# Softmax maxima split on VectorE and moved from SBUF to SBUF, keys in four stored blocks, in a gated cross-attention layer with experts

## The chip, the cores and the metric

The kernel runs on one core of one Trainium2 chip. The metric is the device time of one execution in microseconds. A core has TensorE (PE), VectorE (DVE), ScalarE (ACT), GpSimd (POOL) and SyncE (SP), whose queue issues nearly all DMAs here.

## The reference

Sixteen sequences of 256 tokens with 128 features attend to 1601 context rows each, in 16 heads of depth 8; a mixture of eight experts follows. Both branches are added to x with a tanh gate.

```python
x = x + tanh(g_xattn) * attention(ctx, ctx, layernorm(x))      # qh, kh, vh: heads of 8
#   softmax(qh @ kh.T / sqrt(8)) @ vh, then the dense layer
x = x + tanh(g_ffn) * ffn(layernorm(x))
#   top 2 of 8 experts by sigmoid(x @ gate_W), gelu hidden layers of 64, plus a shared expert
```

## The kernel before

**Steps.** One step is half of a batch's heads: step s works on batch s // 2, eight heads, 256 queries; there are 32 steps. Float32 products of queries and keys are made with bf16 operands: each of q and k is split in three bf16 parts (value, rest, rest of the rest), and 48 rows of an operand tile hold six of their pairings (`KPART`, `QPART`). Two heads' operands lie at partitions 0 and 64 (`SIDE`).

**Two passes over the scores.** For the softmax's maximum, PE computes scores with queries on the partitions (L741, events S, 26 for each step) and DVE reduces them (L901, L904). From these DVE makes the negated maximum of each query and head (`neg_max`, L911). Then PE computes the scores again, transposed, with keys on the partitions (L757, events P, 26 pairs for each step). The negated maximum comes in as three more operand rows, 48 to 50 of each side of `q_op`. ACT takes the exponential of each (L573), PE multiplies with the values (L775, events V and W), and ACT copies the sums out (L581).

**The way of the maxima.** `neg_max` lies with tokens on the partitions; the operand rows need heads on rows and tokens along them. So in event T, PE transposes it (L697), ACT copies it to `nm_t` (L605), POOL splits it in three with four instructions (`split_maxima`, L469 to L475), SP writes the parts to HBM (L416), waits, and reads them back into the rows of `q_op` (L419). The first pair P of the next step waits for that. T of step s+1 stands in step s, after about 17 of its 26 pairs.

**Order.** PE, ACT and DVE each walk one list (`PLAN`, `ORDER`), one string for each phase s % 4. Score passes of step s+1, values of step s and s-1, and auxiliary units are woven in it: K (keys, L688, from `kctx`), V (values, L692, from `vctx`), QT and QP (queries), F (experts), D (dense layer). In the lists of phases 0 and 2 stand the four K units of batch b+2. In phase 0 the first comes at the head, ahead of P0, in phase 2 a little after it; the last comes after T.

**Keys and queries through HBM.** The projected keys `k_t` are split (POOL, four instructions on all 1601 columns, after the last K unit), stored six times over (`store_keys`, L397: 600, 400 and 200 KB for each half) and read back as rows of `k_op` (`load_operands`, L332). Queries go the same way with twelve stores for 512 tokens (L406).

**SP's list.** SP is one queue in program order, and it stops at each wait. In an odd step s it does: outputs of s-1, `store_keys` for b+2, `load_operands` for s+3 (once the stores have landed), key context for b+3 (L387), value context for b+2 (L387, once the last V unit of b+1 is done), maxima of s+1, and in phase 3 the query stores. In an even step: outputs, operands, the softmax's sums by way of HBM (L361, L367), in phase 2 the gates (L375, L381), maxima. Before the loop it issues the context of batch 0, all tokens and weights, `vctx`, the keys of batch 0, `kctx` of batch 1, the queries, the operands of step 0.

## Time and profile before

| what | value |
|---|---|
| median of 3 runs | 1435.47 us (1433.91 to 1437.52) |
| the profiled execution's own time | 1436.73 us |
| its span | 1434.9 us |
| busy, PE / ACT / DVE / POOL | 87% / 74% / 73% / 29% |
| mean granted TensorE clock | 0.902 |
| moved by DMA | 147.13 MB, 103 GB/s |

The span runs from the first to the last instruction of the program. The granted clock is 1.00 at TensorE's 2.4 GHz and 0.50 at 1.2 GHz. In the rows below, a row of the timeline has the start in us, the time that the merged instructions take, the engine, the line of the kernel, the operation with what it writes and reads, and in brackets how long the engine sat idle before it and what ended that.

### The profile page before, as it was taken

Reading aid. Unit: us, or ns where it says so; the run is one execution under the profiler, and the core shown is the slowest. Engines: PE = TensorE matmul, PEld = TensorE weight load, DVE = VectorE, ACT = ScalarE, POOL = GpSimd, SP = SyncE. Lnnn points to the kernel's source line nnn. Section 1 sums busy time; section 2 is a strip of 40 time slices with the busy share of each in tenths; the row PEclk is TensorE's granted clock in tenths of the full one; section 3 lists DMA queues with packets and bytes.
Section 4 is the critical chain, followed back from the end, with each engine's and each line's share of the span. In section 5 each row is a group of like instructions: output and inputs, shape, how many; then the busy total and the mean of one; then the engine's idle time right before and its main releaser. Section 6 shows DMA issues by size and latency. Waiting matters only on the chain.

```text
span 1434.9 us, 29778 instructions
## 1 busy us (share of the span) xinstructions
PE 1241.7 (87%) x11555; PEld 458.9 (32%) x11555; DVE 1049.3 (73%) x1208; ACT 1055.6 (74%) x1962; POOL 418.7 (29%) x309
## 2 busy tenths in 40 slices
PE   2448889798989999899989999799979999799855
PEld 1112323232323433243323333243323433243224
DVE  8477778587768888688868878688768868689001
ACT  1008879587978799688968789688968889689741
POOL 7242224051333215151424125051423205010111
PEclk6568999798988999899989999899989999899786
DMA  7673634636273653737273744637173744501101
GB/s 213 114 149 69 150 70 98 140 84 129 53 164 70 139 119 87 147 81 149 52 169 61 170 87 99 139 82 146 47 167 67 165 92 96 102 11 33 31 14 45
DMA packets 71390, 147.13 MB, mean 103 GB/s; under 512 B 13705, under 2 KB 37970, under 8 KB 71250
## 3 DMA queue, kind: packets, MB, share of 16 engines
q1 hardware_dynamic: 71250, 145.24, 47.4%
q8 instruction: 91, 1.49, 0.5%
q14 instruction: 49, 0.40, 0.1%
HBM read 88.30 MB, written 56.91 MB: 101 GB/s over the span
## 4 chain that ended last, share of the span: by engine, by line
PE 66%; DMA 14%; ACT 5%; DVE 4%; SPq 4%; POOL 3%; issue 2%; POOLq 0%; ACTq 0%; DVEq 0%
PE o_ps L775 26%; PE a_ps L757 15%; PE b_ps L741 11%; DMA m_dram<-nm_parts 10%; PE a_ps L688 4%; PE a_ps L692 4%; ACT probs L573 3%; PE b_ps L720 2%; DVE run_max L901 2%; SPq L406 2%; DMA q_op<-m_dram 1%; SPq L397 1%; PE a_ps L684 1%; PE b_ps L723 1%; DMA q_op<-q_dram 1%
## 5 line engine op out<-in xcount | busy, mean ns | idle before, releaser
L901 DVE TENSOR_REDUCE run_max<-b_ps 128x2 f32<-128x1024 f32 x768 | 899.4, 1218 | 249.4 <-PE b_ps L741 246.0
L573 ACT ACTIVATE probs<-a_ps 128x512 f32<-128x512 f32 (+1 forms) x1664 | 901.9, 594 | 144.3 <-PE a_ps L757 127.4
L775 PE MATMUL o_ps<-probs,v_op 128*32 128x256 f32 (+3 forms) x4928 | 505.8, 483 | 2.3 <-ACT probs L573 1.2
L757 PE MATMUL a_ps<-q_op,k_op 51*128 51x256 bf16 (+1 forms) x3328 | 338.1, 283 | 46.4 <-DMA q_op<-m_dram 25.6
L741 PE MATMUL b_ps<-k_op,q_op 48*128 48x512 bf16 (+1 forms) x2048 | 325.6, 350 | 37.5 <-DVE run_max L901 24.2
L757 PEld LDWEIGHTS a_ps<-q_op,k_op 51*128 51x128 bf16 (+1 forms) x3328 | 112.9, 97 | 373.5 <-ACT probs L573 307.3
L741 PEld LDWEIGHTS b_ps<-k_op,q_op 48*128 48x128 bf16 x2048 | 88.7, 96 | 208.2 <-DVE run_max L901 95.9
L775 PEld LDWEIGHTS o_ps<-probs,v_op 128*32 128x32 f32 (+1 forms) x4928 | 98.4, 109 | 176.4 <-issue 93.8
L509 POOL TENSOR_TENSOR attn<-num,den_all 128x256 f32<-128x256 f32 x16 | 11.6, 728 | 440.3 <-DMA den_all<-r_dram 440.3
L688 PE MATMUL a_ps<-kctx,wk_s 128*128 128x400 f32 (+1 forms) x128 | 81.4, 734 | 55.7 <-DMA kctx<-ctx_t 49.9
L469 POOL TENSOR_TENSOR nm_parts<-nm_t,one 8x256 bf16<-8x256 f32 x32 | 19.3, 602 | 360.5 <-ACT nm_t L605 360.5
L594 ACT ACTIVATE k_t<-a_ps,bk_s 128x401 f32<-128x401 f32 (+1 forms) x64 | 38.1, 597 | 106.7 <-PE a_ps L688 106.6
L692 PE MATMUL a_ps<-wv_s,vctx 128*128 128x128 f32 (+1 forms) x416 | 64.4, 294 | 0.0
L888 DVE SCALAR_TENSOR_TENSOR y_s<-b_ps,tgf,x_s 128x128 f32<-128x128 f32 x32 | 11.2, 349 | 71.3 <-PE b_ps L724 71.2
L599 ACT ACTIVATE v_op<-a_ps 128x512 f32<-128x512 f32 x64 | 32.9, 513 | 36.7 <-PE a_ps L692 36.3
L692 PEld LDWEIGHTS a_ps<-wv_s,vctx 128*128 128x128 f32 (+1 forms) x416 | 51.2, 192 | 20.8 <-issue 11.5
L469 POOL TENSOR_TENSOR k_parts<-k_t,one 128x1601 bf16<-128x1601 f32 x15 | 42.8, 2850 | 43.8 <-ACT k_t L594 43.8
L688 PEld LDWEIGHTS a_ps<-kctx,wk_s 128*128 128x128 f32 x128 | 25.9, 248 | 83.1 <-issue 61.0
L904 DVE TENSOR_REDUCE run_max<-b_ps 128x8 f32<-128x520 f32 x64 | 43.9, 696 | 10.3 <-PE b_ps L741 10.3
L471 POOL TENSOR_TENSOR k_t<-k_t,k_parts 128x1601 f32<-128x1601 f32 x15 | 48.5, 3230 | 1.2
L475 POOL TENSOR_TENSOR k_parts<-k_t,k_parts 128x1601 bf16<-128x1601 f32 x15 | 45.3, 3021 | 1.2
L473 POOL TENSOR_TENSOR k_parts<-k_t,one 128x1601 bf16<-128x1601 f32 x15 | 42.8, 2851 | 1.2
(100 smaller groups left out, 680.4 us busy)
## 6 DMA issues: line engine op xcount, KB each, us to landing
k_op<-k_dram SPq DMA_DIRECT2D x64, 600.4 KB, 9.5
k_dram<-k_parts SPq DMA_DIRECT2D x32, 600.4 KB, 6.0
kctx<-ctx_t SPq DMA_DIRECT2D x16, 800.5 KB, 12.5
vctx<-ctx_t SPq DMA_DIRECT2D x16, 800.5 KB, 11.8
k_dram<-k_parts SPq DMA_DIRECT2D x32, 400.2 KB, 7.0
o_dram<-o_s SPq DMA_DIRECT2D x32, 256.0 KB, 2.1
g_all<-g_dram SPq DMA_DIRECT2D x16, 512.0 KB, 6.4
k_dram<-k_parts SPq DMA_DIRECT2D x32, 200.1 KB, 6.7
```

The costliest lines, as they stand in the source:

```text
L469: pool.tensor_tensor(parts[0], whole, ones(whole, slice(0, whole.shape[0])), ALU.mult).then_inc(chain, 1)
L471: pool.tensor_tensor(whole, whole, parts[0], ALU.subtract).then_inc(chain, 1)
L473: pool.tensor_tensor(parts[1], whole, ones(whole, slice(0, whole.shape[0])), ALU.mult).then_inc(chain, 1)
L475: pool.tensor_tensor(parts[2], whole, parts[1], ALU.subtract).then_inc(chain, 1)
L573: act.activation(probs[0:keys, unit % PB, :], a_ps[at % AB][0:keys, :], ACT.Exp, scale=SCALE).then_inc(a_taken, 1)
L688: last = pe.matmul(bank[:, 0:n_keys], wk_s[:, :], kctx[:, k0:k0 + n_keys], start=True, stop=True)
L692: last = pe.matmul(bank[0:KEYS[t], 128 * (t % 4):128 * (t % 4) + 128], vctx[:, 128 * t:128 * t + KEYS[t]], wv_s[:, :], start=True, stop=True)
L741: last = pe.matmul(slot[:, side, to:to + n_keys], q_op[buf][rows, p, 128 * t:128 * t + 128], k_op[buf][rows, p, k0:k0 + n_keys], start=Tru ...
L757: last = pe.matmul(a_ps[(at + side) % AB][0:KEYS[t], SEQ * a:SEQ * a + SEQ], k_op[buf][rows, slot, 128 * t:128 * t + KEYS[t]], q_op[buf][r ...
L775: last = pe.matmul(o_ps[32 * j:32 * j + 32, cols], v_op[s // 2 % 2][0:KEYS[t], t, GP * (s % 2) + j, :], probs[0:KEYS[t], unit % PB, cols], ...
L901: dve.tensor_reduce(run_max[:, t, :, p, c:c + 1].rearrange("q v o -> q (v o)"), slot[:, :, :], AX.X, ALU.max).then_inc(b_taken, 1)
L904: dve.tensor_reduce(run_max[:, i - FULL, :, :, RUNS], slot[:, :, 0:GP * REST].rearrange("q v (p k) -> q v p k", p=GP), AX.X, ALU.max).then ...
```

## The change

- **Maxima.** DVE splits `neg_max` in three bf16 parts itself, per token, with four more instructions right after L911. Event T is then two bf16 products with an identity, which turn all 24 rows (two sides, three parts, four heads) at once. ACT's copy writes them as bf16 to `nm_t`, and SP moves them straight to the rows of `q_op`, in six DMAs of one row (4 x 256 elements, 2 KB) each. `m_dram` and `split_maxima` are gone.
- **Keys.** The pairings are reordered so that the first three stored parts and one more copy of the first (`KEPT` 4 blocks) do: the last two blocks of rows are read from the first two again. Four stores for each batch instead of six, six operand loads for each step instead of four. The layout in HBM puts the two halves beside each other, so that what a row reads is one stretch of 12.8 KB. POOL splits each K unit's 400 columns when that unit is done; the division of the outputs stands among them.
- **Queries.** Six stores instead of twelve; those of batches 0 and 1 are issued by ACT.
- **SP's list.** In odd steps the maxima come ahead of the key context. The value context of b+1 is loaded in the even step, after the operands.
- **Start.** Only what step 0 needs is issued first; tokens beyond the first 512, the value context and the operands of step 1 come after the operands of step 0. In the lists of steps -2 and -1, five S events come first, then the K and V units, then the rest of step 0's S events and at once T of step 0.

```diff
-KPART = [0, 1, 2, 0, 1, 0]
-QPART = [0, 0, 0, 1, 1, 2]
+KPART = [0, 1, 2, 0, 0, 1]
+QPART = [0, 0, 0, 1, 2, 1]
 SIDE = 64
...
 MROWS = ROWS + 3
-PLACES = [(0, 3), (3, 5), (5, 6)]
+KEPT = 4
+PLACES = [(0, 4), (4, 6)]
+Q_STORED = [(0, 3), (3, 5), (5, 6)]
 PAIR_OF = [0, 2, 1, 3]
...
 S_AHEAD = 10
-OP_DMAS = 4
+OP_DMAS = 2 * (len(PLACES) + 1)
 OUT_DMAS = 3
-PART_STORES = 2 * len(PLACES)
-Q_STORES = 2 * len(QPART)
+MAX_DMAS = 6
+PART_STORES = 4
+Q_STORES = 2 * len(Q_STORED)
 FIRST, LAST = -2, 4 * CHUNKS + 5
...
 GATE_OPS = 12
+DIVIDE_AT = [3, 2]
...
+def first_maxima():
+    scores = [event for event in ORDER[-2] if event[0] == "S"]
+    rest = [event for event in ORDER[-2] if event[0] != "S"]
+    first = [event for event in ORDER[-1] if event[0] == "S" and event[1] < SUNITS]
+    turn = [("A", ("T", 0, 0))]
+    return scores[:5] + rest + scores[5:], first + turn + [e for e in ORDER[-1] if e not in first + turn]
+ORDER[-2], ORDER[-1] = first_maxima()
...
-        k_dram = nc.dram_tensor("k_dram", [2, 2, len(KPART), 64, CTX], BF16, kind="Internal").ap()
-        m_dram = nc.dram_tensor("m_dram", [2, 3, 2 * GP, SEQ], BF16, kind="Internal").ap()
+        q_dram = nc.dram_tensor("q_dram", [CHUNKS, len(QPART), 64, 2, CHUNK], BF16, kind="Internal").ap()
+        k_dram = nc.dram_tensor("k_dram", [2, KEPT, 64, 2, CTX], BF16, kind="Internal").ap()
         r_dram = nc.dram_tensor("r_dram", [2 * GP, 2, SEQ], F32, kind="Internal").ap()
...
         neg_max = sb("neg_max", [128, QTILES, 2 * GP])
-        nm_t = sb("nm_t", [2 * GP, SEQ])
-        nm_parts = sb("nm_parts", [2 * GP, 3, SEQ], BF16)
+        nm_parts = sb("nm_parts", [128, QTILES, 2, 3, GP], BF16)
+        nm_t, ident_b = sb("nm_t", [6 * GP, SEQ], BF16), sb("ident_b", [128, 128], BF16)
...
             else:
-                engine.wait_ge(k_chain, 4 * b)
+                engine.wait_ge(k_chain, 4 * len(KRUN) * b)
+        def store_queries(engine, c):
+            engine.wait_ge(q_chain, 4 * (c + 1))
+            for a in range(2):
+                for r0, r1 in Q_STORED:
+                    parts = q_parts[64 * a:64 * a + 64, QPART[r0]:QPART[r0] + 1, :].broadcast_to([64, r1 - r0, CHUNK]) \
+                        if QPART[r0] == QPART[r1 - 1] else q_parts[64 * a:64 * a + 64, QPART[r0]:QPART[r1 - 1] + 1, :]
+                    engine.dma_start(q_dram[c, r0:r1, :, a].rearrange("n r q -> r n q"), parts).then_inc(q_written, 16)
...
                 load(dst, src).then_inc(key_in, 16)
-            sp.dma_start(x_s[:, 0:4, :], x[:, 0:4, :]).then_inc(x0_in, 16)
+            def load_tokens(c0, c1, arrived):
+                for c in range(c0, c1):
+                    sp.dma_start(x_s[:, 4 * c:4 * c + 4, :], x[:, 4 * c:4 * c + 4, :]).then_inc(arrived, 16)
+            load_tokens(0, 1, x_in[0])
             for dst, src in firsts:
...
                 load(dst, src).then_inc(const_in, 16)
-            for c in range(1, CHUNKS):
-                sp.dma_start(x_s[:, 4 * c:4 * c + 4, :], x[:, 4 * c:4 * c + 4, :]).then_inc(x_in, 16)
...
+                kd = k_dram[b % 2].rearrange("n (d p) a c -> (n d) p a c", p=PAIRS)
+                qd = q_dram[b // 2, :, :, :, SEQ * (b % 2):SEQ * (b % 2) + SEQ].rearrange("n (d p) a q -> (n d) p a q",
+                                                                                       p=PAIRS)
                 for side in range(2):
...
                     pairs = slice(GP * g + 2 * side, GP * g + 2 * side + 2)
-                    sp.dma_start(k_op[buf][rows, :, :].rearrange("r (a p) c -> r a p c", a=2),
-                                 kd[:, :, pairs, :]).then_inc(op_in[buf], 16)
-                    sp.dma_start(q_op[buf][rows, :, :].rearrange("r (a p) q -> r a p q", a=2),
-                                 qd[:, :, pairs, :]).then_inc(op_in[buf], 16)
+                    for r0, r1 in PLACES:
+                        to = slice(SIDE * side + DH * r0, SIDE * side + DH * r1)
+                        sp.dma_start(k_op[buf][to, :, :], kd[0:DH * (r1 - r0), pairs]
+                                     .rearrange("r p a c -> r (p a) c")).then_inc(op_in[buf], 16)
+                    sp.dma_start(q_op[buf][rows, :, :],
+                                 qd[:, pairs].rearrange("r p a q -> r (p a) q")).then_inc(op_in[buf], 16)
...
-                        sp.dma_start(k_dram[b % 2, a, r0:r1].rearrange("n r c -> r n c"),
-                                     k_parts[64 * a:64 * a + 64, 0:r1 - r0, :]).then_inc(k_written, 16)
-            def store_queries(c):
-                sp.wait_ge(q_chain, 4 * (c + 1))
-                for a in range(2):
-                    for part, (r0, r1) in enumerate(PLACES):
-                        for r in range(r0, r1):
-                            sp.dma_start(q_dram[2 * c:2 * c + 2, a, r].rearrange("b r q -> r b q"),
-                                         q_parts[64 * a:64 * a + 64, part, :]
-                                         .rearrange("p (b q) -> p b q", b=2)).then_inc(q_written, 16)
+                    rows = slice(64 * a, 64 * a + 64)
+                    sp.dma_start(k_dram[b % 2, 0:3, :, a].rearrange("n r c -> r n c"),
+                                 k_parts[rows, :, :]).then_inc(k_written, 16)
+                    sp.dma_start(k_dram[b % 2, 3, :, a], k_parts[rows, 0, :]).then_inc(k_written, 16)
...
-                h = s % 2
-                sp.wait_ge(m_chain, 4 * (s + 1))
-                if s >= 2:
-                    sp.wait_ge(m_in[h], 32 * (s // 2))
-                sp.dma_start(m_dram[h].rearrange("n h q -> h n q"), nm_parts[:, :, :]).then_inc(m_written, 16)
-                sp.wait_ge(m_written, 16 * (s + 1))
+                sp.wait_ge(a_taken, a_done("T", s))
                 for side in range(2):
-                    sp.dma_start(q_op[s % 4][SIDE * side + ROWS:SIDE * side + MROWS, :, :],
-                                 m_dram[h, :, GP * side:GP * side + GP, :]).then_inc(m_in[h], 16)
+                    for n in range(3):
+                        row, col = SIDE * side + ROWS + n, 3 * GP * side + GP * n
+                        sp.dma_start(q_op[s % 4][row:row + 1, :, :], nm_t[col:col + GP, :]).then_inc(m_in[s % 2], 16)
+            store_keys(0)
+            load_operands(0)
+            load_context("K", kctx, 1, kctx_in)
+            load_tokens(1, 2, x_in[1])
+            load_operands(1)
             load(vctx, ctx_t[0]).then_inc(vctx_in, 16)
-            store_keys(0)
-            load_context("K", kctx, 1, kctx_in)
-            store_queries(0)
-            load_operands(0)
+            load_tokens(2, CHUNKS, x_in[2])
             for s in range(FIRST, LAST + 1):
...
                     move_outputs(s - 1)
-                if s % 2 == 1 and b + 2 < BATCH:
+                if s % 2 == 1 and 0 < b + 2 < BATCH:
                     store_keys(b + 2)
-                if 0 <= s + 3 < STEPS:
+                if 2 <= s + 3 < STEPS:
                     load_operands(s + 3)
+                if s % 2 == 0 and 0 < b + 1 < BATCH:
+                    load_context("V", vctx, b + 1, vctx_in)
                 if s % 2 == 0 and 0 <= b - 1 < BATCH:
...
                     spread_gates((s - 6) // 4)
-                if s % 2 == 1 and b + 3 < BATCH:
-                    load_context("K", kctx, b + 3, kctx_in)
-                if s % 2 == 1 and 0 <= b + 2 < BATCH:
-                    load_context("V", vctx, b + 2, vctx_in)
                 if 0 <= s + 1 < STEPS:
                     move_maxima(s + 1)
+                if s % 2 == 1 and 0 < b + 3 < BATCH:
+                    load_context("K", kctx, b + 3, kctx_in)
                 if s % 4 == 3 and 0 < (s + 5) // 4 < CHUNKS:
-                    store_queries((s + 5) // 4)
+                    store_queries(sp, (s + 5) // 4)
                 if s % 4 == 1 and 0 <= (s - 9) // 4 < CHUNKS:
...
-                pool.wait_ge(a_taken, a_done("K", b, 3))
-                pool.wait_ge(k_written, 16 * PART_STORES * b)
-                split3(k_chain, 4 * (b - 1), k_t[:, :], [k_parts[:, i, :] for i in range(3)])
+            def split_keys(b, i):
+                pool.wait_ge(a_taken, a_done("K", b, i))
+                if i == 0:
+                    pool.wait_ge(k_written, 16 * PART_STORES * b)
...
                     apply_gates((s - 7) // 4)
-                if s % 2 == 0 and 0 <= b - 1 < BATCH:
-                    divide(b - 1)
-                if 0 <= s + 1 < STEPS:
-                    split_maxima(s + 1)
-                if s % 2 == 0 and b + 2 < BATCH:
-                    split_keys(b + 2)
+                for i in range(len(KRUN)):
+                    if s % 2 == 0 and i == DIVIDE_AT[s % 4 // 2] and 0 <= b - 1 < BATCH:
+                        divide(b - 1)
+                    if s % 2 == 0 and 0 < b + 2 < BATCH:
+                        split_keys(b + 2, i)
                 if s % 4 == 3 and 0 < (s + 5) // 4 < CHUNKS:
...
                     if n > 0:
-                        act.wait_ge(m_chain, 4 * n)
-                    op = act.activation(nm_t[:, :], bank[0:2 * GP, 0:SEQ], ACT.Copy)
+                        act.wait_ge(m_in[(n - 1) % 2], 16 * MAX_DMAS * ((n - 1) // 2 + 1))
+                    op = act.activation(nm_t[:, :], bank[0:6 * GP, 0:SEQ], ACT.Copy)
                 elif kind in ("QT", "FT"):
...
                 aux_unit(*unit)
+            store_queries(act, 0)
             act.wait_ge(const_in, 16 * len(consts))
...
+                    pe.wait_ge(ident_cast, 1)
                     pe.wait_ge(nm_ready, n + 1)
                     for t in range(QTILES):
-                        last = pe.transpose(bank[0:2 * GP, 128 * t:128 * t + 128], neg_max[:, t, :], ident[:, :])
+                        last = pe.matmul(bank[0:6 * GP, 128 * t:128 * t + 128],
+                                         nm_parts[:, t].rearrange("q v n p -> q (v n p)"), ident_b[:, :],
+                                         start=True, stop=True)
                 last.then_inc(a_filled, 1)
...
                 for a in range(2):
-                    slot = 2 * a + i % GP // 2
+                    slot = 2 * (i % GP // 2) + a
                     for side in range(2):
...
-                dve.wait_ge(x_in, 16 * (CHUNKS - 1))
...
-                                      ALU.max, negate=True).then_inc(nm_ready, 1)
+                                      ALU.max, negate=True).then_inc(nm_seq, 1)
+                    whole = neg_max[:, :, :].rearrange("q t (v p) -> q t v p", p=GP)
+                    parts = [nm_parts[:, :, :, part, :] for part in range(3)]
+                    dve.wait_ge(nm_seq, 4 * s + 1)
+                    dve.tensor_copy(parts[0], whole).then_inc(nm_seq, 1)
+                    dve.wait_ge(nm_seq, 4 * s + 2)
+                    dve.tensor_tensor(whole, whole, parts[0], ALU.subtract).then_inc(nm_seq, 1)
+                    dve.wait_ge(nm_seq, 4 * s + 3)
+                    dve.tensor_copy(parts[1], whole).then_inc(nm_seq, 1)
+                    dve.wait_ge(nm_seq, 4 * s + 4)
+                    dve.tensor_tensor(parts[2], whole, parts[1], ALU.subtract).then_inc(nm_ready, 1)
...
-            dve.wait_ge(x0_in, 16)
+            dve.wait_ge(x_in[0], 16)
             statistics("q", 0)
...
             dve.memset(hid_s[:, :], 1.0).then_inc(v_ones, 1)
+            dve.wait_ge(first_in, 16 * len(firsts))
+            dve.tensor_copy(ident_b[:, :], ident[:, :]).then_inc(ident_cast, 1)
             fold_bias()
...
                         if s % 4 == 2 and n == 2 and 0 < (s + 6) // 4 < CHUNKS:
+                            if s < 4:
+                                dve.wait_ge(x_in[s // 4 + 2], 16 if s < 0 else 16 * (CHUNKS - 2))
                             statistics("q", (s + 6) // 4)
...
```

## Rows read from the trace of the kernel before

**Rows 1.** The page, busy us, share of the span, instructions:
```profile
PE 1241.7 (87%) x11555; PEld 458.9 (32%) x11555; DVE 1049.3 (73%) x1208; ACT 1055.6 (74%) x1962; POOL 418.7 (29%) x309
```

**Rows 2.** Waits: who waited for whom, us in total, times, longest:
```profile
PE a_ps L688 <- DMA kctx<-ctx_t: 49.9, 8, 9.0
...
PE a_ps L757 <- DMA q_op<-m_dram: 25.6, 15, 7.2
```

**Rows 3.** Timeline, the end of step 7 and the start of step 8:
```profile
396.40 9.22 SPq L397 DMA_DIRECT2D k_dram<-k_parts  x6
...
408.77 1.23 DVE L901 TENSOR_REDUCE run_max<-b_ps 128x2 f32<-128x1024 f32 x1 [0.73 <-PE b_ps L741]
...
409.88 0.38 PE L697 MATMUL a_ps<-ident,neg_max 128*8 128x128 f32 x2
409.92 0.33 SPq L332 DMA_DIRECT2D k_op<-k_dram  x1
...
413.54 0.29 SPq L416 DMA_DIRECT2D m_dram<-nm_parts  x1
...
425.39 1.68 PE L688 MATMUL a_ps<-kctx,wk_s 128*128 128x401 f32 x2 [6.35 <-DMA kctx<-ctx_t]
426.02 0.58 SPq L419 DMA_DIRECT2D q_op<-m_dram  x2
...
427.80 0.61 PE L757 MATMUL a_ps<-q_op,k_op 51*128 51x256 bf16 x4 [0.19 <-DMA q_op<-m_dram]
```

**Rows 4.** A window: busy PE, PEld, DVE, ACT, POOL; clock, DMA share, GB/s:
```profile
120.00:1340.00 1220.00, 1132.48 (x10938) 412.14 (x10936) 960.88 (x1088) 998.76 (x1859) 360.02 (x271) 0.94 0.49 104
```

**Rows 5.** Windows, exponentials on ACT alone: busy (count), clock, DMA share, GB/s:
```profile
427.80:440.30 12.50, 5.33 (x10) 0.50 0.41 99
...
303.10:315.60 12.50, 9.50 (x18) 1.00 0.46 106
...
1109.30:1121.80 12.50, 8.68 (x16) 1.00 0.41 97
```

**Rows 6.** DMA issues in windows 408:414, 0:2, 498:500: KB, us to landing:
```profile
k_op<-k_dram SPq DMA_DIRECT2D x2, 600.4 KB, 8.5
kctx<-ctx_t SPq DMA_DIRECT2D x1, 800.5 KB, 13.5
...
kctx<-ctx_t SPq DMA_DIRECT2D x1, 800.5 KB, 4.7
...
vctx<-ctx_t SPq DMA_DIRECT2D x1, 800.5 KB, 7.5
```

**Rows 7.** Timeline, the end of step 17 and the start of step 18:
```profile
814.17 0.35 SPq L387 DMA_DIRECT2D vctx<-ctx_t  x1
...
824.99 0.39 PE L757 MATMUL a_ps<-q_op,k_op 51*128 51x256 bf16 x4 [2.38 <-DMA q_op<-m_dram]
```

**Rows 8.** Timeline of SP's queue in step 8:
```profile
450.49 1.28 SPq L367 DMA_DIRECT2D den_all<-r_dram  x2
458.26 0.28 SPq L416 DMA_DIRECT2D m_dram<-nm_parts  x1
459.64 0.56 SPq L419 DMA_DIRECT2D q_op<-m_dram  x2
```

**Rows 9.** Source lines: shortest, median, longest ns, first and last start:
```profile
L846 DVE TENSOR_SCALAR score<-score x8: 170/170/173, 322.1 to 1405.8; 128x32 f32<-128x32 f32 x8
...
L834 DVE TENSOR_TENSOR rstd_f<-mv_f,eps_f x8: 163/1011/2751, 300.4 to 1395.8; 128x4 f32<-128x4 f32 x8
```

**Rows 10.** Timeline of the start:
```profile
20.97 9.31 SPq L397 DMA_DIRECT2D k_dram<-k_parts  x6
...
42.29 0.35 SPq L332 DMA_DIRECT2D k_op<-k_dram  x1
...
54.16 1.03 PE L741 MATMUL b_ps<-k_op,q_op 48*128 48x512 bf16 x4 [12.48 <-DMA q_op<-q_dram]
...
110.81 0.61 PE L757 MATMUL a_ps<-q_op,k_op 51*128 51x256 bf16 x4 [1.52 <-DMA q_op<-m_dram]
```

22 lines of the change are left out of this document (7 added, 15 removed).

## The prediction

> **What bounds the kernel now.** I read the page first. TensorE is busy for 87% of the span, VectorE and ScalarE for about 73% [rows 1]. So PE's order sets the time, and 193 us (1434.9 less 1241.7) are its idle time. The view of waits says what ended that idle time: the key context's transfer 49.9 us in 8 waits, the maxima's last transfer 25.6 us in 15 waits [rows 2]. Two of the 8 lie before and in step 0. The other six come once in four steps.
>
> The timeline of one of the six shows the mechanism [rows 3]. T of step 8 is transposed at 409.88. SP issued the key stores from 396.40 on and is let go when they have landed. It then issues the operands (409.92), the key context, the value context, and at 413.54 the maxima's way to HBM. All of it shares the DMA engines: the operands take 8.5 us, and the key context lands 13.5 us after its issue [rows 6], which was thus near 411.7 or T + 1.8. PE runs out of work at 419.04 (425.39 less 6.35), which is T + 9.2 us. It restarts at 425.39 for the K unit, and P0 starts at 427.80. Both the context and the maxima are late there, by some 6 and some 7 us. Without either lateness P0 would come 2.4 us after K, at T + 11.6.
>
> Each stall has a second price. The clock after it is 0.50 (1.2 GHz) for some 12 us: ScalarE makes 10 exponentials in 12.5 us, against 18 and 16 at 1.00 [rows 5]. That is 0.59 of the mean of 17, so a microsecond at the lower level costs 0.41 us. Over the steady part the clock's mean is 0.94 [rows 4], which is 0.06 / 0.5 x 1220 = 146 us at the lower level. It starts while PE still idles, and idle time is counted by itself; I take 128 us as worked through, between 85 (all idle time taken off) and 146.
>
> **The odd steps' maxima.** Before: T, 3.66 us of copy and split, a transfer to HBM, one back. Where the engines are free, the first takes 1.38 us up to SP's next issue [rows 8]; behind the contexts it was 12.48 us (426.02 less 413.54). After: T, ACT's copy (about 0.8 us to its end), six issues at 0.28 us each (0.56 for two [rows 8]) = 1.7 us, and one landing. P0 ran 1.8 us after the pair of issues began at 426.02 [rows 3], so I take 1.5 to 2 us for a landing from SBUF to SBUF as well (the change's kind of transfer is in no row; below it is bounded by nothing but the issue, above by the 1.38 + 1.8 us of both). Sum: T + 4.3 us. Needed is T + 9 to T + 11.6. POOL's four splits and the HBM trip are gone from the path. In steps 1 mod 4 SP also waited for the last V unit before the value context (issued 814.17; PE idle 2.38 us ahead of P0 at 824.99 [rows 7]); this wait leaves the odd steps.
>
> For this the rings must be free when the maxima are issued. The key stores shrink from 2400 to 1600 KB for each batch. The 2400 KB took 13.5 us, from 396.40 to 409.92 [rows 3]; at that rate 1600 KB need 9 us, and the keys of the last K unit are split 9 us earlier on POOL. The operands are then issued 4 to 6 us earlier, about T - 6, and drained by T + 2.5 (8.5 us [rows 6]).
>
> **The key context** is now issued behind the six maxima, at T + 2.7 instead of T + 1.8, but with no operands ahead and no value context beside it. Its landing took 4.7 us in the quiet start, the value context's 7.5 us with a tail of traffic ahead [rows 6]. So it lands at T + 7.4 to T + 10.2, where PE wants it at T + 9.2. I allow 0 to 1 us of idle time, and 8 us over all.
>
> **The terms.**
> - Idle time: six context waits like the one of 6.35 = 38 us, and 25.6 less the first of 1.52 [rows 10] = 24 us of waits for maxima, the longest (7.2) in step 28, which loads no keys. Together 62 us go.
> - Clock: 128 x 0.41 = 52 us. Bounds 85 x 0.36 (10 against 16) = 31 and 146 x 0.44 (10 against 18) = 64.
> - What stays of the context's lateness: -8. Bounds 0 and the whole 71 (below).
> - DVE's four instructions: 0.17 us each for small tiles [rows 9], 0.7 us with their waits, 32 times = 22 us if DVE paced PE there. After L911 DVE idles 0.73 us before its next but one reduction [rows 3], which absorbs most; in steps 1 mod 4 the gate's small instructions follow and nothing absorbs it. Queued behind them are the reductions that free the score slots for PE. I take -10, bounds 0 and -22.
> - T on PE: 0.38 us in float32 [rows 3]; bf16 products of 256 columns run four in 0.39 us at full clock [rows 7], so two of 128 cost about 0.1. +6, bounds 0 (another engine paces) and +9.
> - Start: +8, below. POOL's splits by run: 0; they lie beside other work, and the last K unit's split needs 3 us instead of 12. Fewer query stores: 0, hidden after the maxima. The value context in even steps: 0, cover named in the last rival.
> - End: nothing changes from the last exponential on: 0.
>
> Of L834 the row shows 1.0 us in the median and 2.75 at most, where it takes 0.16 undisturbed, with POOL's 3 us key splits running beside it [rows 9]. The Trainium skill (SBUF — State Buffer, Who interferes with whom) says that DVE and GpSimd share a port pair as an exclusive lock, so that a DVE instruction with two SBUF inputs waits for a whole GpSimd instruction; the trace agrees. By that rule the four new instructions could each wait for a POOL instruction; with POOL busy 29% and its key instructions cut to a quarter, the sum would hardly change.
>
> **Start.** Before: the last split at 20.9, six key stores from 20.97 to 30.28, the next context, twelve query stores, operands at 42.29, first scores at 54.16, P0 at 110.81 [rows 10]. After: 1600 KB of keys and 768 KB of queries (ACT's queue beside SP's) from 21 on, at that same rate: 34; operands 8.5 us: 42.5. So the scores start 11 to 12 us earlier. Then they wait in PE's list for the value context, which now stands behind the operands of step 1: 4.6 MB from 34 on. In the steady part 104 GB/s go at a DMA share of 0.49 [rows 4], which is some 210 for a full one, so it lands near 57. The 21 S events left, at DVE's 1.2 us each, end near 84, T at 87. P0 follows after ten S events of step 1 near 102, the maxima and the context having landed. That is 8 us of gain, bounds 0 and 20.
>
> **Sum.** 62 + 52 + 8 + 6 - 10 - 8 = 110 us. The profiled span becomes 1434.9 - 110 = 1325; its own time was 1.8 us above the span and the median of the runs shown 1.3 us below that own time. So I predict 1325 us.
>
> **Rivals.**
> 1. *The key context takes the place of the wait.* If stores or operands are not drained at T, it lands late. Missing by 2.4 us, as the maxima did in [rows 7], costs 2.4 + 7 x 0.41 = 5.3 us in six steps: 1325 less the 8 allowed, plus 32, is 1349. If it lands after 13.5 us as before, the idle time is 7 us with the clock's 5: 1388. Middle 1360. For it: the margin is -1 to +2 us, and the context moved behind six issues. Against: 0.8 to 1.6 MB less stands ahead and beside.
> 2. *DVE becomes the bound*: all 22 us exposed and some port waits on top, and the S events pace each step at 1.2 us: 1340 to 1350.
> 3. *Six small transfers do not overlap.* Each then costs its 1.8 us: the maxima land at T + 12, P0 waits 1 to 3 us in half of the steps, with the clock's price: about 1375. Against it, two issued in 0.56 us were both in after one 1.8 us. The Trainium skill (DMA: Bandwidth & Descriptors, Rules for kernel authors) advises to join small transfers, since under 64 KB one pays mostly overhead; here three transfers of 6 to 12 KB become six of 2 KB. By its fixed cost of about 2 us the sum would be as in this rival if the cost were paid in a row, and as in mine if side by side.
> 4. *Slower: the even steps stall.* The value context (800 KB) now stands ahead of the softmax's sums, on which SP waits before the maxima. Before, SP was done with them at 451.8, and T was at 454.6 (458.26 less 3.66) [rows 8]. The 800 KB add 4 to 7 us to that wait: maxima at T + 2 to T + 4, landing by T + 8, needed at about T + 11.6. To cost all 110 us, 16 even steps must lose 7 us each, 4 idle and 3 by the clock: maxima landing at T + 16, 8 us later than the worst of this. From a delay of 16 us on it decides; then 1440 or more.
> 5. *No change*: the context keeps 13.5 us and the start, too, stays as it is; that still leaves the waits of steps 2 mod 4 and 28 gone, so it needs the even steps to lose as well: 1435.
>
> **How the numbers follow.** My forecast with its terms' bounds (1300 to 1345) 0.67, rival 1 0.17, rival 2 0.06, rival 3 0.05, rival 4 0.03, no change 0.02. The range for 8 in 10 takes in the forecast, rival 2 and the nearer half of rival 1: 1298 to 1368. A measurement of this kernel tells 0.3% (4.3 us) from no change: faster 0.95, within it 0.02, slower 0.03.
>
> **What would show it.** Right: PE's waits for the maxima near nothing; those for the key context under 10 us behind step 0; the clock's mean over the steady part 0.98 or more; SP's six issues within 3 us of T; first scores near 42 and P0 near 102. Wrong: a K unit that idles PE for more than 1 us once in four steps, with the clock at 0.50 behind it (rival 1); score products that wait on DVE right after T (rival 2); maxima that land 10 us after T (rival 3) or SP held by the sums when T is done (rival 4). The likeliest error is the context's margin, next the clock's term: it may be that shorter stalls still drop it.

## The result and the profile after

The changed kernel takes 1332.0 us in the median of four runs (1326.53 to 1340.7), the kernel before 1436.14 in four runs of the same comparison. The ratio is 0.928, with a 95% interval from 0.922 to 0.934: 7.2% faster. The prediction was 1325 us in a range from 1298 to 1368. The profiled execution took 1328.48 us with a span of 1326.7, so the profile stands 3.5 us below the median and accounts for 108 us of the difference of spans (1434.9 less 1326.7).

The page of the changed kernel: busy time by engine, the granted clock in 40 slices, and two groups of DMA issues with their size and the median us to landing.

```profile
PE 1194.2 (90%) x11555; PEld 452.9 (34%) x11555; DVE 1060.7 (80%) x1337; ACT 1056.2 (80%) x1962; POOL 370.6 (28%) x361
...
PEclk7567999899999999999999999999999999899876
...
k_op<-k_dram SPq DMA_DIRECT2D x64, 400.2 KB, 7.1
...
kctx<-ctx_t SPq DMA_DIRECT2D x16, 800.5 KB, 4.9
```

The same transfers on the page of the kernel before:

```profile
k_op<-k_dram SPq DMA_DIRECT2D x64, 600.4 KB, 9.5
...
kctx<-ctx_t SPq DMA_DIRECT2D x16, 800.5 KB, 12.5
```

PE has 132 us of idle time in its span where it had 193 [rows 1]. Its busy time also fell, by 47 us, with the same 11555 matmuls: more of them ran at the upper clock. That is the second price of a stall, seen from the other side.

The waits say which idle time went (who waited for whom, us, times, longest):

```profile
PE b_ps L758 <- DVE run_max L917: 30.6, 58, 1.9
...
PE a_ps L702 <- DMA kctx<-ctx_t: 6.5, 5, 2.0
...
PE a_ps L706 <- DMA vctx<-ctx_t: 4.9, 1, 4.9
```

The key context's 49.9 us in 8 waits [rows 2] are 6.5 us in 5, and no score product waits for the maxima any more. The window of the steady part (columns as in [rows 4]) has the clock at 0.99:

```profile
120.00:1240.00 1120.00, 1083.07 (x10920) 404.64 (x10914) 968.04 (x1209) 999.00 (x1860) 303.10 (x303) 0.99 0.47 101
```

The end of step 7 and the start of step 8, the place of [rows 3], in the timeline:

```profile
370.44 0.65 SPq L427 DMA_DIRECT2D k_dram<-k_parts  x1
...
379.96 1.07 SPq L362 DMA_DIRECT2D k_op<-k_dram  x2
...
385.98 0.27 PE L712 MATMUL a_ps<-ident_b,nm_parts 128*24 128x128 bf16 x2
...
386.74 3.79 SPq L437 DMA_DIRECT2D q_op<-nm_t  x6
390.58 0.44 SPq L417 DMA_DIRECT2D kctx<-ctx_t  x1
...
397.23 0.91 PE L702 MATMUL a_ps<-kctx,wk_s 128*128 128x401 f32 x2 [2.00 <-DMA kctx<-ctx_t]
...
398.30 0.38 PE L774 MATMUL a_ps<-q_op,k_op 51*128 51x256 bf16 x4
```

Read it from T at 385.98. The stores begin at T - 15.5 and the operands are issued at T - 6.0. Before, the stores began at T - 13.5 and the operands were issued as T began (409.92 and 409.88 [rows 3]). So 4 of these 6 us come from shorter stores, and 2 from their earlier start. The six maxima are issued from T + 0.8 to T + 4.6, so the key context is issued at T + 4.6 and PE, out of work at 395.23 (T + 9.25), waits 2.0 us for it. P0 at 398.30 waits for no maxima. This short wait leaves the clock alone: it is 1.00 in the 12.5 us behind it.

```profile
397.20:409.70 12.50, 12.43 (x118) 4.06 (x118) 10.55 (x10) 11.15 (x21) 10.14 (x12) 1.00 0.50 104
```

### The profile page after: what moved, and what is told of

It is laid out like the page before. It is cut to its first block, busy times and chain, and to the rows that moved or that the text cites. A ratio compares the mean times of both kernels' runs of the same rounds, so it can differ in the third digit from the quotient of the medians.

```text
span 1326.7 us, 29978 instructions
## 1 busy us (share of the span) xinstructions
PE 1194.2 (90%) x11555; PEld 452.9 (34%) x11555; DVE 1060.7 (80%) x1337; ACT 1056.2 (80%) x1962; POOL 370.6 (28%) x361
## 4 chain that ended last, share of the span: by engine, by line
PE 72%; DVE 13%; DMA 5%; ACT 4%; issue 3%; SPq 1%; POOL 1%; ACTq 1%; POOLq 0%; DVEq 0%
PE o_ps L792 27%; PE a_ps L774 16%; PE b_ps L758 13%; DVE run_max L917 8%; PE a_ps L702 4%; PE a_ps L706 4%; ACT probs L586 3%; PE a_ps L698 2%; DMA kctx<-ctx_t 2%; PE b_ps L737 2%; DVE run_max L920 2%; DMA vctx<-ctx_t 1%; PE b_ps L726 1%; PE a_ps L682 1%; ACTq L321 1%
## 5 line engine op out<-in xcount | busy, mean ns | idle before, releaser
L792 PE MATMUL o_ps<-probs,v_op 128*32 128x256 f32 (+3 forms) x4928 | 490.5, 470 | 2.3 <-ACT probs L586 1.2
L758 PE MATMUL b_ps<-k_op,q_op 48*128 48x512 bf16 (+1 forms) x2048 | 321.0, 343 | 41.2 <-DVE run_max L917 30.6
L774 PE MATMUL a_ps<-q_op,k_op 51*128 51x256 bf16 (+1 forms) x3328 | 328.3, 276 | 21.7 <-ACT probs L586 17.5
L488 POOL TENSOR_TENSOR k_parts<-k_t,one 128x400 bf16<-128x400 f32 (+1 forms) x60 | 51.2, 853 | 185.1 <-ACT k_t L607 185.1
L499 POOL TENSOR_TENSOR rstd_q<-rstd_q,minus_half 128x4 f32<-128x4 f32 x8 | 8.1, 1011 | 270.7 <-DVE rstd_q L850 270.7
L702 PE MATMUL a_ps<-kctx,wk_s 128*128 128x400 f32 (+1 forms) x128 | 67.0, 617 | 12.3 <-DMA kctx<-ctx_t 6.5
L904 DVE SCALAR_TENSOR_TENSOR y_s<-b_ps,tgf,x_s 128x128 f32<-128x128 f32 x32 | 11.1, 348 | 70.3 <-PE b_ps L741 70.2
L490 POOL TENSOR_TENSOR k_t<-k_t,k_parts 128x400 f32<-128x400 f32 (+1 forms) x60 | 56.8, 947 | 4.7
L494 POOL TENSOR_TENSOR k_parts<-k_t,k_parts 128x400 bf16<-128x400 f32 (+1 forms) x60 | 53.6, 893 | 4.7
L492 POOL TENSOR_TENSOR k_parts<-k_t,one 128x400 bf16<-128x400 f32 (+1 forms) x60 | 50.9, 849 | 4.7
L612 ACT ACTIVATE v_op<-a_ps 128x512 f32<-128x512 f32 x64 | 32.9, 516 | 15.8 <-PE a_ps L706 15.5
L534 POOL TENSOR_TENSOR hid<-hid,g_all 128x2048 f32<-128x2048 f32 x8 | 36.3, 4533 | 30.6 <-DMA g_all<-g_dram 20.7
```

Of the source, the lines that this page charges most:

```text
L488: pool.tensor_tensor(parts[0], whole, ones(whole, slice(0, whole.shape[0])), ALU.mult).then_inc(chain, 1)
L490: pool.tensor_tensor(whole, whole, parts[0], ALU.subtract).then_inc(chain, 1)
L492: pool.tensor_tensor(parts[1], whole, ones(whole, slice(0, whole.shape[0])), ALU.mult).then_inc(chain, 1)
L494: pool.tensor_tensor(parts[2], whole, parts[1], ALU.subtract).then_inc(chain, 1)
L702: last = pe.matmul(bank[:, 0:n_keys], wk_s[:, :], kctx[:, k0:k0 + n_keys], start=True, stop=True)
L758: last = pe.matmul(slot[:, side, to:to + n_keys], q_op[buf][rows, p, 128 * t:128 * t + 128], k_op[buf][rows, p, k0:k0 + n_keys], start=Tru ...
```

## The experiments

Each kernel was timed beside the kernel before; the ratio to it has its 95% interval in brackets. Kernels of one group ran on the same chip; the changed kernel was timed in a comparison of its own, so it stands against them by its ratio and its spans. "Span" is that of the profiled execution.

### First group: the two suspects and the order of SP's queue

**The changed kernel with its maxima moved as before.** The keys, the queries' stores, the order and the start stay changed; T is a float32 turn again, POOL splits, and the maxima go by HBM.

```diff
-                sp.wait_ge(a_taken, a_done("T", s))
-                for side in range(2):
-                    for n in range(3):
-                        row, col = SIDE * side + ROWS + n, 3 * GP * side + GP * n
-                        sp.dma_start(q_op[s % 4][row:row + 1, :, :], nm_t[col:col + GP, :]).then_inc(m_in[s % 2], 16)
+                sp.wait_ge(m_chain, 4 * (s + 1))
...
+                sp.dma_start(m_dram[h].rearrange("n h q -> h n q"), nm_parts[:, :, :]).then_inc(m_written, 16)
+                sp.wait_ge(m_written, 16 * (s + 1))
+                for side in range(2):
+                    sp.dma_start(q_op[s % 4][SIDE * side + ROWS:SIDE * side + MROWS, :, :],
+                                 m_dram[h, :, GP * side:GP * side + GP, :]).then_inc(m_in[h], 16)
...
+            def split_maxima(s):
+
+                pool.wait_ge(a_taken, a_done("T", s))
```

> The changed kernel with the maxima's old way (float32 turn, split on GpSimd, to HBM and back); all else stays changed. Theory (the waits came from transfers queued ahead, not from the trip itself): on free rings the old trip lands near T + 8, inside the T + 9 to T + 11.6 that TensorE needs, but the key context is issued only when the trip to HBM has ended, near T + 6.5, and misses by 2 us in six steps: 1340 to 1355. Rival (the split on GpSimd and the HBM trip were the loss): most of the gain is gone, 1400 or more, with waits for the maxima of 2 us and more at the head of all steps 0 and 2 mod 4.

Measured: 1326.95 us, 0.926 [0.920, 0.932], span 1326.7: not slower than the changed kernel, and no wait for the maxima. The rival falls. The theory's mechanism stands, but not its 1340 to 1355. At the end of step 7 the old way reads so:

```profile
380.87 0.38 PE L725 MATMUL a_ps<-ident,neg_max 128*8 128x128 f32 x2
...
384.52 0.28 SPq L438 DMA_DIRECT2D m_dram<-nm_parts  x1
387.52 0.56 SPq L441 DMA_DIRECT2D q_op<-m_dram  x2
388.12 0.36 SPq L418 DMA_DIRECT2D kctx<-ctx_t  x1
...
392.58 1.28 PE L716 MATMUL a_ps<-kctx,wk_s 128*128 128x401 f32 x2 [2.55 <-DMA kctx<-ctx_t]
...
394.20 0.63 PE L785 MATMUL a_ps<-q_op,k_op 51*128 51x256 bf16 x4
```

From the write to the reads it is 3.0 us, where it was 12.48 in [rows 3], and the last read is issued at T + 7.2. Here the operands went out ahead of T and no context stands ahead of the maxima; in [rows 3] the operands and both contexts did. The key context goes out at T + 7.3 and is 2.55 us late, as the theory had it. But the changed kernel has nearly the same lateness (7.9 us in 5 waits here, 6.5 in 5 there), so it was no reason to be slower.

**The kernel before with the new way of the maxima alone** (the same edit turned round).

> The kernel before with the new way of the maxima alone (split on VectorE, SBUF to SBUF); keys, queue order and start stay old. Theory: the key context still lands 13 us after its issue behind the operands and beside the value context, so the six waits of some 6 us and their clock price stay; only the waits in steps 2 mod 4 and step 28 shrink: 1400 to 1415. Rival (the way of the maxima is the main part of the change): 1350 to 1370.

Measured: 1419.9 us, 0.989 [0.981, 0.996], span 1421.5, a little above the 1415 expected. The new way is worth about 16 us where the rings are full (by the interval 6 to 27). The maxima's waits fall from 25.6 us to 11.4, and the context waits stay:

```profile
PE a_ps L674 <- DMA kctx<-ctx_t: 58.2, 8, 12.0
...
PE a_ps L746 <- DMA q_op<-nm_t: 11.4, 5, 6.4
```

At the end of step 7 the context is issued at 421.52, ahead of the maxima, and PE idles for it all the same:

```profile
421.52 0.53 SPq L386 DMA_DIRECT2D kctx<-ctx_t  x1
...
422.59 3.80 SPq L415 DMA_DIRECT2D q_op<-nm_t  x6
...
435.14 1.68 PE L674 MATMUL a_ps<-kctx,wk_s 128*128 128x401 f32 x2 [6.32 <-DMA kctx<-ctx_t]
```

**The changed kernel with the key context issued ahead of the maxima.**

```diff
-                if 0 <= s + 1 < STEPS:
-                    move_maxima(s + 1)
                 if s % 2 == 1 and 0 < b + 3 < BATCH:
                     load_context("K", kctx, b + 3, kctx_in)
+                if 0 <= s + 1 < STEPS:
+                    move_maxima(s + 1)
```

> The changed kernel with the key context issued ahead of the maxima in odd steps. Theory: the operands are drained by then, the context is issued near T - 3 instead of T + 5 and has landed when the maxima are issued; the 6.5 us of waits for the context go with what clock they cost, and the maxima stay in time: 1320 to 1330, some 5 to 8 us faster than the changed kernel. Rival (small transfers suffer from any large one ahead of them): waits for the maxima of 1 to 3 us come back in half of the steps, 1340 to 1360.

Measured: 1317.72 us, 0.919 [0.914, 0.924], span 1315.6, which is 11.1 us below the changed kernel's, somewhat more than the 5 to 8 expected. No wait for the key context is left behind the start, and the clock is 1.00:

```profile
120.00:1220.00 1100.00, 1072.00 (x10874) 402.11 (x10870) 967.20 (x1208) 991.27 (x1846) 299.32 (x303) 1.00 0.48 103
```

**The same, with the value context, too, ahead of the maxima in the odd steps**, as in the kernel before (the edit is against the kernel with the key context first).

```diff
-                if s % 2 == 0 and 0 < b + 1 < BATCH:
-                    load_context("V", vctx, b + 1, vctx_in)
...
                 if s % 2 == 1 and 0 < b + 3 < BATCH:
                     load_context("K", kctx, b + 3, kctx_in)
+                if s % 2 == 1 and 0 < b + 2 < BATCH:
+                    load_context("V", vctx, b + 2, vctx_in)
                 if 0 <= s + 1 < STEPS:
                     move_maxima(s + 1)
```

> The changed kernel with both contexts issued ahead of the maxima in odd steps, as in the kernel before; in steps 1 mod 4 SP then waits for the last V unit again. Theory: 800 KB more lie ahead of the maxima, which land near T + 9 to T + 11; TensorE waits 0 to 2 us at P0 in steps 2 mod 4 and less in steps 0 mod 4, clock included some 15 to 30 us slower than the changed kernel: 1345 to 1360. Rival (queue order does not matter once the maxima no longer pass HBM): 1326 to 1335.

Measured: 1326.38 us, 0.925 [0.919, 0.930], span 1323.2. The theory's 15 to 30 us over the changed kernel are missing; this expectation was a miss. Two contexts ahead of the maxima cost 8 to 9 us more than one (by spans and by medians; the runs of the two kernels do not overlap, the intervals do), not a stall in each batch. In neither kernel does PE wait for a context or for the maxima in the steady part. The mean clock of the profiled executions is 0.945 against 0.952, some 19 us more at the lower level (0.055 / 0.5 x 1323.2 less 0.048 / 0.5 x 1315.6), which at the prediction's 0.41 would be 8 us. That is an estimate, and what lowered the clock stays open.

### Second group: the keys

**The changed kernel with six stored blocks of keys** (2400 KB for each batch and loads of 48 rows; layout, split by run and all else as changed).

```diff
-KEPT = 4
-OP_DMAS = 2 * (len(PLACES) + 1)
-PART_STORES = 4
+KEPT = 6
+OP_DMAS = 4
+PART_STORES = 6
...
+                    sp.dma_start(k_dram[b % 2, 4:6, :, a].rearrange("n r c -> r n c"),
+                                 k_parts[rows, 0:2, :]).then_inc(k_written, 16)
```

> The changed kernel with six stored blocks of keys instead of four (one load of 48 rows for each side again; the split by run and the layout stay). Theory K, formed on e1 and e4 (what freed TensorE is that fewer and earlier key stores let the operands go before T): the 2400 KB cost some 4.5 us more, operands go near T - 1, the key context lands near T + 12 and TensorE waits 2 to 3 us for it in six steps, with the clock: 1350 to 1370. Theory O (it is the order in SP's queue, the value context out of the odd steps and the maxima ahead): 1326 to 1335.

Measured: 1373.14 us, 0.959 [0.955, 0.962], span 1375.5: 41 us slower than the changed kernel in the median, and just above the range of theory K. Theory O falls. The stall is back:

```profile
PE a_ps L702 <- DMA kctx<-ctx_t: 23.2, 6, 5.1
```

```profile
385.09 0.65 SPq L425 DMA_DIRECT2D k_dram<-k_parts  x1
...
398.62 0.32 SPq L360 DMA_DIRECT2D k_op<-k_dram  x1
...
400.59 0.28 PE L712 MATMUL a_ps<-ident_b,nm_parts 128*24 128x128 bf16 x2
...
405.21 0.44 SPq L415 DMA_DIRECT2D kctx<-ctx_t  x1
...
413.45 1.00 PE L702 MATMUL a_ps<-kctx,wk_s 128*128 128x401 f32 x2 [3.62 <-DMA kctx<-ctx_t]
```

The stores begin at T - 15.5, as in the changed kernel, but last 13.5 us (385.09 to 398.62) instead of 9.5 (370.44 to 379.96). So the operands are issued at T - 2.0 instead of T - 6.0, and are still on the rings when the context comes. The window shows the second price, a clock of 0.97 where the changed kernel has 0.99:

```profile
120.00:1280.00 1160.00, 1108.20 (x10955) 409.80 (x10954) 974.45 (x1214) 998.91 (x1858) 304.31 (x309) 0.97 0.51 108
```

**The changed kernel with POOL's split of the keys in one piece** behind the last K unit, and **both together.**

```diff
-                cols = slice(KRUN[i][0], KRUN[i][0] + KRUN[i][1])
-                split3(k_chain, 4 * (len(KRUN) * (b - 1) + i), k_t[:, cols], [k_parts[:, n, cols] for n in range(3)])
+                split3(k_chain, 4 * (b - 1), k_t[:, :], [k_parts[:, i, :] for i in range(3)])
```

> The changed kernel with the keys of batches 2 and up split by GpSimd on all 1601 columns after the last K unit, as before. Theory K: the stores start 2 us later in steps 3 mod 4, some of the margin of the key context goes: 1332 to 1345. Theory O: no difference, 1326 to 1335.

> Both of these together: keys stored in six blocks and split whole; maxima, SP's order, layout, queries and start stay changed. Theory K: 1360 to 1385, more than half of the stalls' gain lost. Theory O: 1326 to 1340.

Measured: 1337.68 us (0.935 [0.928, 0.941], span 1330.3) for the split alone, whose interval overlaps the changed kernel's; 1396.7 us (0.976 [0.971, 0.981], span 1392.6) for both, 12 us above the range expected, with more of the same wait:

```profile
PE a_ps L699 <- DMA kctx<-ctx_t: 35.4, 6, 7.1
```

With the split alone the stores begin at T - 13.4 (371.14, T at 384.52), yet the waits for the key context are 3.8 us in 4, against 6.5 in 5 in the changed kernel: with four blocks the 2 us lost there do not show. From the kernel with both on, four blocks alone take off 59 us (1396.7 to 1337.68), the split by run alone 24 (to 1373.14), and both 65 (to 1332.0). Either remedy does part of the other's work, and the blocks do the larger part.

**The reverse: the kernel before with the keys' and the queries' part of the change alone**, that is four blocks, the split by run, the new layout and six stores of queries; maxima, queue order and start as before.

> The reverse of e10: keys in four blocks, split by run and laid out anew, and the six query stores; maxima by way of HBM, both contexts ahead of the maxima and the start as in the kernel before. Theory K: most of the gain is there, 1340 to 1365. Theory O: 1400 or more, with the waits of the kernel before.

Measured: 1316.85 us, 0.919 [0.915, 0.924], span 1322.6. This one part gives the whole gain, where 1340 to 1365 was expected for most of it. By the medians it is even 15 us faster than the whole change, though the intervals (0.915 to 0.924, 0.922 to 0.934) just overlap. At step 8:

```profile
370.40 1.08 SPq L364 DMA_DIRECT2D k_op<-k_dram  x2
...
373.41 0.44 SPq L419 DMA_DIRECT2D kctx<-ctx_t  x1
...
387.08 0.58 SPq L442 DMA_DIRECT2D q_op<-m_dram  x2
...
388.92 0.46 PE L783 MATMUL a_ps<-q_op,k_op 51*128 51x256 bf16 x4 [2.06 <-DMA q_op<-m_dram]
```

The context goes out right behind the operands, 13.7 us ahead of the maxima's last issue, and its only waits lie at the start (8.1 us in 2). What is left is P0's wait for the maxima, 10.5 us in 8.

### Third group: the start, VectorE, and the best version

**The changed kernel with the old start**: the value context and the tokens at their old places, no list of first maxima.

```diff
-ORDER[-2], ORDER[-1] = first_maxima()
...
+            load_tokens(1, 2, x_in[1])
+            load_tokens(2, CHUNKS, x_in[2])
...
+            load(vctx, ctx_t[0]).then_inc(vctx_in, 16)
             store_keys(0)
-            load_operands(0)
             load_context("K", kctx, 1, kctx_in)
-            load_tokens(1, 2, x_in[1])
-            load_operands(1)
-            load(vctx, ctx_t[0]).then_inc(vctx_in, 16)
-            load_tokens(2, CHUNKS, x_in[2])
+            load_operands(0)
```

> The changed kernel with the old start: tokens and the value context issued first, one operand load ahead, the old order of the lists in steps -2 and -1. The reordered start was predicted to gain 8 us; e11 with the old start had P0 of step 0 at 102.3, the changed kernel at 106.3. Theory (the new start costs, since the value context comes late and VectorE waits for it): P0 near 102, 1322 to 1330. Rival (the 102.3 of e11 came from its other parts): P0 near 110, 1332 to 1340.

Measured: 1317.9 us, 0.919 [0.914, 0.923], span 1313.5. P0 of step 0 stands at 98.11; in the changed kernel it is at 106.31. The new start costs 8.2 us there, of 13.2 us of span; the other 5 are not explained, and the intervals of the two kernels just overlap. Both the time and P0 came in below the 1322 and the 102 expected. The new start has its first scores sooner (44.72 against 49.16), and then this:

```profile
44.72 1.03 PE L758 MATMUL b_ps<-k_op,q_op 48*128 48x512 bf16 x4 [10.11 <-DMA q_op<-q_dram]
...
58.87 2.04 PE L706 MATMUL a_ps<-wv_s,vctx 128*128 128x128 f32 x8 [4.92 <-DMA vctx<-ctx_t]
...
64.16 2.36 DVE L917 TENSOR_REDUCE run_max<-b_ps 128x2 f32<-128x1024 f32 x2 [11.58 <-PE b_ps L758]
...
106.31 0.63 PE L774 MATMUL a_ps<-q_op,k_op 51*128 51x256 bf16 x4
```

The scores stop behind the V units, whose context SP issued at 39.92 behind twelve operand transfers, the key context and a load of tokens; VectorE, which paces the maxima, has nothing to do for 11.58 us.

**The changed kernel with four more small VectorE instructions in each step**, copies of the split into tiles that nobody reads, in the same chain and ahead of the real split.

```diff
+                    dve.tensor_copy(more[0], whole).then_inc(nm_seq, 1)
+                    dve.wait_ge(nm_seq, 8 * s + 2)
+                    dve.tensor_tensor(nm_more[:, :, :, :], whole, more[0], ALU.subtract).then_inc(nm_seq, 1)
+                    dve.wait_ge(nm_seq, 8 * s + 3)
+                    dve.tensor_copy(more[1], nm_more[:, :, :, :]).then_inc(nm_seq, 1)
+                    dve.wait_ge(nm_seq, 8 * s + 4)
+                    dve.tensor_tensor(more[2], nm_more[:, :, :, :], more[1], ALU.subtract).then_inc(nm_seq, 1)
```

> The changed kernel with four more small VectorE instructions of the same kinds after the maxima of each step, results unused. Theory (VectorE paces TensorE after the maxima, and little of this is absorbed, as the step lengths of 34.4 and 37.1 against 33.7 to 34.0 and 36.0 to 36.4 in e1 suggest): 0.5 to 0.9 us in three of four steps, 12 to 25 us slower than the changed kernel, 1342 to 1356. Rival (VectorE's idle time absorbs it): 1326 to 1335.

Measured: 1356.78 us, 0.946 [0.941, 0.951], span 1353.7: 25 us more in the median, 0.78 us in each of 32 steps. That is nearly their whole length: four of 0.17 us, 0.21 us from start to start, 0.84 us together. T, too, comes later by that, but behind the start no PE instruction waits for T's operands or for the maxima it sends. The waits for VectorE's reductions grew from 30.6 us in 58:

```profile
PE b_ps L759 <- DVE run_max L918: 50.6, 66, 2.5
```

**Key context first and maxima by HBM**, and **the same with the old start.** Of the change, the last keeps the keys, the queries' stores and the value context in the even steps.

> e1 (maxima by their old way through GpSimd and HBM, all else changed) with the key context issued ahead of the maxima. Theory: no wait for the context and none for the maxima, which land near T + 7.4, and VectorE has four instructions less: 10 to 20 us below e3's 1318 is the steady part's promise, 1300 to 1312. Rival (behind the context the HBM trip is late): waits of 1 to 2 us at P0 as in e11, 1315 to 1330.

> e12 with the old start as well, so that of the change only the keys, the query stores and the value context's place in even steps are left, with the key context ahead of the maxima as before. Theory: 3 to 5 us below e12, 1296 to 1308, the fastest of all. Rival: the same as e12.

Measured: 1311.67 us (0.914 [0.910, 0.918], span 1312.0), and 1306.1 us (0.910 [0.906, 0.914], span 1304.2), the fastest of all and 26 us below the changed kernel. Its steady part has no transfer in PE's idle time:

```profile
120.00:1210.00 1090.00, 1069.16 (x10792) 399.62 (x10790) 941.08 (x1076) 984.28 (x1839) 380.75 (x427) 1.00 0.49 104
```

## Why the prediction was right, and where it was not

**The mechanism held.** Stores that finish earlier let the operands out earlier, and then little is late at the end of step 3 mod 4: no maxima, and the key context by 2 us or less. The terms were 13.5 us and 9 us for the stores, T - 6 for the operands, T + 9.2 for PE's want; measured are 13.5 (six blocks), 9.5, T - 6.0 and T + 9.25. Putting back the two blocks raised the waits for the key context from 6.5 to 23.2 us and the time by 41. Of the last K unit's split, 9 us earlier on POOL by the prediction, 2 us arrived at the stores' start.

**The clock's term held.** The clock's mean rose from 0.94 to 0.99, as predicted 0.98 or more. By the prediction's own reckoning, 0.01 / 0.5 x 1120 = 22 us are left at the lower level of 146, so 124 x 0.41 = 51 us came back; taken were 52. The six blocks agree with the price: the steady part is longer by about 42 us (48.8 us of span less 7 at P0 of step 0), of which 16.7 are added waits for the context and 1.8 one for the maxima, and 0.03 / 0.5 x 1160 less 22 is 48 us more at the lower level, 20 us at 0.41. That makes 38 of the 42. The two places of the mean are coarse: half a hundredth is 11 us at the lower level, or 5 us of time. The doubt about shorter stalls is answered at two places: behind the wait of 2.00 us the clock stays at 1.00, but behind the 2.55 us in the kernel with the maxima's old way it is 0.59:

```profile
392.50:405.00 12.50, 12.42 (x59) 3.32 (x62) 6.17 (x6) 6.98 (x13) 8.23 (x10) 0.59 0.50 119
```

**The sum.** Of 110 us the span shows 108. Before P0 of step 0 it is 4.5 (110.81 less 106.31) where 8 were taken; the rest is 103.7, where 62 + 52 + 6 - 10 - 8 = 102 were taken.

**The credit for the maxima was wrong.** I ascribed 24 of the 62 us, and their share of the clock, to the maxima's new way ("POOL's four splits and the HBM trip are gone from the path"). The maxima's waits did vanish, but the keys alone take them from 25.6 us to 10.5 and give the whole gain (1316.85 us), and the old way put back costs nothing (1326.95 against 1332.0). It is worth 16 us only while the rings are full. Both halves of the change act on one cause, the queue of transfers at T: what the new way saves alone, the keys save too, and most of what the keys save the new way can't reach. [Rows 8] already had it: 1.38 us with the rings free against 12.48 in [rows 3].

**The issue cost was mis-sized.** "Six issues at 0.28 us each = 1.7 us" were 3.79 us. The 0.28 came from reads of three rows out of HBM, and the new ones are of one row from SBUF. So the key context was issued at T + 4.6, not T + 2.7. The wait it cost, 2.0 us at this place, is beyond the 0 to 1 allowed, and over all it is 6.5 us in 5. And SP's six issues end at T + 4.6, where "within 3 us of T" was the sign of being right. The price follows from putting the context first: 11.1 us of span, 6.5 of them idle time; the other 4.6 I put down to the clock (0.99 against 1.00), which two places can't prove. The term was -8, bounds 0 and 71. By medians it is 14 us, but the two intervals (0.914 to 0.924, 0.922 to 0.934) just overlap.

**VectorE's term held for the first four instructions only.** Taken were -10 for them and +6 for the shorter T, -4 together. The HBM way undoes both (and gives POOL its splits back): with the key context first in both kernels it is 3.6 us of span faster (1315.6 against 1312.0), 6 us in the medians, which is not clear of the noise (0.910 to 0.918, 0.914 to 0.924). The first term shows by itself in PE's waits for VectorE's reductions behind the start: 2.6 us in 7 with the HBM way and 12.2 in 29 with the four instructions, 9.6 us more where 10 was taken. The second four raise them, in the same stretch, from the changed kernel's 11.7 to 30.6 and cost 25 us. So the slack that I read in [rows 3], 0.73 us of VectorE idle beside the turn, exists once. T on PE was mis-sized: the two bf16 products take 0.27 us where 0.1 was taken and 0.38 was before, so 32 times 0.11 is 3.5 us and not 6. The bound of 22 us for four instructions that nothing absorbs was near the 25 measured for the second four. Rival 2 is thus near: at this place further VectorE work is paid nearly in full.

The timeline of VectorE at T of step 8 shows the four, with no gap ahead of the reductions:

```profile
381.58 0.22 DVE L927 TENSOR_REDUCE neg_max<-run_max 128x16 f32<-128x64 f32 x1
381.83 0.17 DVE L933 CAST nm_parts<-neg_max 128x16 bf16<-128x16 f32 x1
...
382.46 0.17 DVE L939 TENSOR_TENSOR nm_parts<-neg_max,nm_parts 128x16 bf16<-128x16 f32 x1
382.74 3.49 DVE L917 TENSOR_REDUCE run_max<-b_ps 128x2 f32<-128x1024 f32 x3
```

Of the port lock (the Trainium skill, SBUF — State Buffer, Who interferes with whom) the new instructions show nothing: the longest of the 32 at L935, with two SBUF inputs, took 0.176 us, but GpSimd has no instruction beside any of them (it is busy for 0.00 us from 381.50 to 382.70), so the rule wasn't put to the test there.

**The start's gain did not come from the start's edit.** The sum took "+8" for the start, of which 4.5 came. The predicted first scores (42.5) and value context (near 57) were measured at 44.7 and 58.9, T at 88.2 for 87. P0 came 4 us late because a V unit of 4.08 us and the Q turns stand between T and P0, and I had counted the ten S events alone. But with the old start P0 stands at 98.1, 12.7 us earlier than before, and the new start gives 8.2 of them back. With the keys' part alone it is at 102.3, which is 8.5 us from that part. I had written down the idle time of VectorE up to the value context and not asked what the old place of that context would give.

**The rivals.** Rival 1 (context late) came in a small form inside the forecast's bounds; with six blocks it came in full, at 1373 where 1349 to 1388 had been said. Of its sign, a K unit that waits for more than 1 us, half was seen (2.00 us), but not the clock at 0.50 behind it. Rival 3 (six transfers in a row) did not: the Trainium skill's advice to join small transfers (DMA: Bandwidth & Descriptors, Rules for kernel authors) bears on their issue here, 3.79 us instead of 0.56, and not on their landing. With the key context first, the six go out from 381.81 on and P0 starts at 391.33 without a wait, 9.5 us later, where six times 1.8 us in a row would be 10.8. Rival 4 did not come either; no even step waits for maxima.

**Open.** The layout of the stored keys and queries and the queries' six stores were not tried apart from the block count in the kernel before. Six blocks and the split in one piece, put back together, give back 65 us of the 104 between 1332.0 and 1436.14. Between the kernel with the new maxima alone (1419.9) and the one with six blocks split in one piece (1396.7) lie the layout, the query stores, the contexts' order and the new start, 23 us together, not told apart. Why the clock is lower with two contexts ahead of the maxima than with one was not looked into.

## What to carry to other kernels

When two different transfers are both late at one place, look for what stands ahead of both: shrink or advance that first, and price the second remedy only on the kernel in which the first is done. On a queue, put the transfer that is wanted first ahead of a row of small ones, and price a small transfer's issue from a row of its own kind. A slack that one group of instructions fits into is gone for the next, which a doubled group shows in one run.

## What was not expected of the hardware

- Six transfers of one row from SBUF to SBUF hold SP for 3.79 us, 0.63 us each; two reads of three rows from HBM hold it for 0.56. Their landings overlap and their issues do not.
- Bulk stores hold the issuing queue, too: with six stores in a row (the kernel with six blocks) SP's first two take 0.65 and 0.61 us, and the third and those behind it mostly 1.6 to 2.5. These are the second, the third and the last:

```profile
385.79 0.61 SPq L427 DMA_DIRECT2D k_dram<-k_parts  x1
386.44 2.27 SPq L428 DMA_DIRECT2D k_dram<-k_parts  x1
...
392.03 2.46 SPq L428 DMA_DIRECT2D k_dram<-k_parts  x1
```
